# VectorE empties the projections' bank behind the first maximum of the next run in place of in front of it

## Chip, core and metric

The kernel runs on one core of one Trainium2 chip. The metric is the device time of one execution in microseconds (us), the median of several; lower is better. The core's engines work side by side, each through its own list in order, and wait for one another by semaphores: TensorE (PE in the profile, PEld for its weight loads), VectorE (DVE), ScalarE (ACT), GpSimd (POOL), and SyncE's DMA queue (SP).

## What is computed

Four layers of transformer blocks over x of 8 batches x 512 tokens x 256 features, float32. Seven stages hold the first three layers: self-attention (causal), cross-attention, MLP, cross-attention, self-attention with a mask that is loaded, cross-attention, MLP. The last stage is a causal self-attention with 16 heads of 64. The five attention stages that matter here have 16 heads of 16 features and share one form:

```python
h = _ln(x, ln2_g, ln2_b)
q = _heads(_lin(h, q_w, q_b))
k = _heads(_lin(enc_out, k_w, k_b))
v = _heads(_lin(enc_out, v_w, v_b))
a = _attend(q, k, v, causal=False)      # softmax(q k^T * scale) v
x = x + _lin(a, ca_proj_w, ca_proj_b)
```

## The kernel before

An attention stage is cut into 16 units: 8 batches, each in two halves of 8 heads. While one unit's probabilities are computed, the maxima of the next unit's scores are found; its keys, queries and values come from projections that run one or two units ahead. The function `slot(u, ...)` of each engine writes what that engine does in one unit's time, and all engines walk through the same numbered places. A unit has 32 score tiles, k = 0 to 31, in short runs of three (`RUNS[False]`, places r = 0 to 10), or of two in the stage with a loaded mask (`RUNS[True]`, r = 0 to 15).

For each tile TensorE writes the scores for the maximum into one of three banks called `MX` (tile k into bank k % 3), and the scores for the exponential into one of three banks `ST`. VectorE reduces each MX bank to a column of `mx` (L1255 in the cross stages, L1252 in the causal stage, L1248 with the loaded mask, where it also adds the mask to every second ST tile, L1262). TensorE may write MX tile k only when the maximum of tile k - 3 is done, the tiles of the unit before included:

```python
wait(pe, mx_red, TILES * (U if k >= RING else U - 1) + before(k) + 1)
```

Behind the tiles of a run TensorE does jobs at places of a table, `AT`: products with the values (`OUT`), and jobs that all write one single bank, `L`. Each L job waits (`begin`) until the job before it in L has been read out (`l_free`). `K` and `Q` are the key and query projections; ScalarE reads them first (`hi`), then VectorE (`lo`, L1274). `T0` and `T1` turn normalized rows (L618), `M0` and `M1` turn the maxima (L754); ScalarE reads these. In a unit of the second half TensorE projects values at places `V0` and `V1` and VectorE reads them out (`values_out`, L1281, into `V`). In a unit of the first half it projects the attention's output at `O0` and `O1` and VectorE adds them to X (`output_sum`, L1194). For runs of three V0 and O0 lie at place 7, M0 at 8, V1 and O1 at 9, T0 at 10; for runs of two at 11, 9, 13 and 15. So the tile behind V0 and O0 is k = 24, and behind V1 and O1 k = 30 (runs of three) or 28 (runs of two).

Below, "V unit" is a unit with V0 and V1, and "O unit" one with O0 and O1. They take turns. There are 40 of each in the five stages, 80 units with 160 such read-outs.

Of the kernel before, what the change touches and what calls it, by code (L numbers as in the profile page):

```python
# [73 lines left out]
def program(nc, x_in, ctx_in, ctx_rows_in, masks_in, shapes_in, cols_in, rows_in, wts, out):  # L74
# [12 lines left out]
    with es:  # L87
        def sb(name, shape, dt=F32):
            return es.enter_context(nc.sbuf_tensor(name, shape, dt))
# [14 lines left out]
        V = sb("V", [P, 2, NT * H * 32])  # L104
# [114 lines left out]
        def wait(eng, s, v):  # L219

            if not isinstance(v, int) or v > 0:
                eng.wait_ge(s, v)
# [31 lines left out]
        def prob_at(k):  # L254

            return prob[:, k % (4 * G), :]

        def tail_of(s, u):

            return ATTN[s][2], lagged(s, u)  # L260
# [8 lines left out]
        def xt(b, t, n=1):  # L269

            return X[:, bass.ds(NT * b + t, n), :]
# [37 lines left out]
        def a_of(s, u, b):  # L309

            return (s + 1, b + 1 - NB) if isinstance(u, int) and u >= UNITS - 2 else (s, b + 1)

        def m_of(s, u):

            return s + 1 if isinstance(u, int) and u == UNITS - 1 else s

        def end_of(s, u, b):

            return (s - 1, NB - 1) if isinstance(u, int) and u == 0 else (s, b - 1)


        def norm_of(s, u):

            if u == -2:
                return s, 0
            if u % 2 and (u + 1 < UNITS - 2 or s + 1 in JOINED and u < UNITS):
                return a_of(s, u + 1, (u + 1) // 2)
            return None
# [5 lines left out]
        L_NO = {}  # L334
# [835 lines left out]
        def _(dve):  # L1170
            def statistics(N, rows, t):

                if t == 0:
                    wait(dve, ln_mv, NT * N)
                nc.vector.bn_stats(st6[:, t, :], rows).then_inc(ln_stats, 1)

            def combine(N):

                waits(dve, (xh_ready, N), apart=True)
                for t in range(NT):  # L1180
                    waits(dve, (ln_stats, NT * N + t + 1), apart=True)
                    nc.vector.bn_aggr(mv[:, t, :], st6[:, t, :]).then_inc(ln_mv, 1)
# [6 lines left out]
            def layer_norm_x(N, b):  # L1189
                layer_norm(N, lambda t: xt(b, t))  # L1190

            def add_to_x(b, j, bank, done):

                nc.vector.tensor_tensor(xt(b, 2 * j, 2), bank, xt(b, 2 * j, 2), ALU.add).then_inc(done, 1)  # L1194

            def attention(s):
                cross, causal, addmask = ATTN[s]
                n = ATTN_NO[s]

                def slot(u, c, b, p, on):  # L1200
                    half, par = c % 2, c // 2
                    U, GB = UNITS * n + u, NB * n + b
                    sa, _ = a_of(s, u, b)
                    se, be = end_of(s, u, b)
                    norm = norm_of(s, u)
                    if u == UNITS - 2 and on["a"]:
                        prepare(s + 1)
                    if u == -2:
                        layer_norm_x(NB * sa, 0)
                    place = AT[addmask]  # L1210
                    for r, run in enumerate(RUNS[addmask]):
                        for k in run:
                            if on["m"] and k % 16 == 0:
                                wait(dve, max_split, 2 * (U + 1) - 3 + k // 16)
                            if on["m"]:
                                max_tile(m_of(s, u), U + 1, 1 - half, k)
                            if on["b"] and addmask and k % G in BY_VECTOR:
                                add_mask(u, U, k)
                            if on["a"] and k == run[0] and r - 1 in (place["K1"], place["Q"]):
                                low_part(sa, U, half, int(r - 1 == place["Q"]))  # L1220
                        if u != -2 and norm is not None and r < 2:
                            sn, bn = norm
                            if r == 0 and sn > 0:
                                wait(dve, x_done, NB * (sn - 1) + bn + 1)
                            for t in (2 * r, 2 * r + 1):
                                statistics(NB * sn + bn, xt(bn, t), t)
                        if u != -2 and norm is not None and r == place["combine"]:
                            combine(NB * norm[0] + norm[1])
                        if on["tail"] and r == place["invert"] + (tail_of(s, u) == (False, True)):
                            invert(U, 1 - half)  # L1230
                        for part in range(2):
                            if half == 0 and on["op"] and r == place[f"O{part}"]:
                                output_sum((se, be), L_NO[s, u, f"O{part}"], part)
                            if half == 1 and on["a"] and r == place[f"V{part}"]:
                                values_out(sa, u, 1 - par, part)

                def output_sum(end, job, part):

                    dve.wait_ge(l_full, job + 1)
                    add_to_x(end[1], part, Lt, l_free)  # L1240

                def max_tile(sm, U, half, k):
                    _, causal, addmask = ATTN[sm]
                    qt = k % NT
                    waits(dve, (mx_full, TILES * U + k + 1), apart=addmask or causal)
                    bank, m = MXB[k % RING], mx[:, half, k:k + 1]
                    if addmask:
                        nc.vector.tensor_tensor_reduce(bank[:, :], bank[:, :], mask_q[:, qt, :], 1.0, -3.0e38,  # L1248
                                                       ALU.add, ALU.max, m).then_inc(mx_red, 1)
                    elif causal:  # L1250
                        k_n = P * (qt + 1)
                        nc.vector.tensor_tensor_reduce(bank[:, 0:k_n], bank[:, 0:k_n], later0[:, S - k_n:S], 1.0, -3.0e38,  # L1252
                                                       ALU.add, ALU.max, m).then_inc(mx_red, 1)
                    else:
                        nc.vector.tensor_reduce(m, bank[:, :], AX.X, ALU.max).then_inc(mx_red, 1)  # L1255

                def add_mask(u, U, k):
                    i = k // G
                    if k % G == 0:
                        wait(dve, pv_done, 8 * U + i - 3)  # L1260
                    dve.wait_ge(st_full, TILES * U + k + 1)
                    nc.vector.tensor_tensor(prob_at(k), STB[k % RING], mask_k[:, i % 4, :], ALU.add).then_inc(st_masked, 1)  # L1262

                def invert(U, half):

                    for g in range(2):
                        dve.wait_ge(few_in[g], 16 * U)
                    nc.vector.reciprocal(few[:, half, :], few[:, half, :]).then_inc(recip_done, 1)

                def low_part(sa, U, half, kind):  # L1270

                    dve.wait_ge(hi_done, 2 * (U + 2) + kind + 1)
                    at = (C_K, C_Q)[kind] + 2 * ATTN_NO[sa] + half
                    nc.vector.scalar_tensor_tensor(lo[:, kind, :], L[:, :], cols[:, at:at + 1], hi[:, kind, :].bitcast(F32),  # L1274
                                                   ALU.add, ALU.subtract).then_inc(l_free, 1)

                def values_out(sa, u, vpar, j):
                    dve.wait_ge(l_full, L_NO[s, u, ("V0", "V1")[j]] + 1)
                    to = Vh[:, vpar, 2 * j:2 * j + 2, :, :].rearrange("p t h (d two) -> p t h d two", two=2)[:, :, :, :, 0]
                    bias = brow[:, sa % 2, 0:1, :].rearrange("p t (h d) -> p t h d", h=H).broadcast_to([P, 2, H, HD])  # L1280
                    nc.vector.tensor_tensor(to, Lt.rearrange("p t (h d) -> p t h d", h=H), bias, ALU.add).then_inc(l_free, 1)  # L1281

                run_slots(dve, s, slot)

            def mlp(s):
# [180 lines left out]
            def prepare(s):  # L1466

                dve.wait_ge(brow_in[s % 2], brow_count(s))
                if s == CROSS1:
                    quantize()  # L1470
                    dve.wait_ge(quant, QUANT_STEPS)
                scale_queries(s, W[s % 2][:, 0:512], HD ** -0.5)
                if addmask_of(s):
                    dve.wait_ge(masks_loaded, 32)
# [333 lines left out]
```

## Time and profile before

| | us |
|---|---|
| time, median of 3 runs | 4148.82 (4137.39 to 4149.97) |
| span of the profiled execution, first to last instruction | 4128.6 |
| TensorE busy in the span | 3800.3 (92%) |
| VectorE busy | 2734.4 (66%) |
| ScalarE busy | 2398.9 (58%) |
| GpSimd busy | 1660.8 (40%) |

The profiled execution has no time of its own beside its span. The median lies 20.2 us above the span; this is taken as what lies around the instructions. In the span the five attention stages run from about 80 to 1000 us (causal, then cross), from 1220 to 1730 us (cross), to 2290 us (loaded mask) and to 2830 us (cross), the MLPs between them, and the last stage from there to the end. In the rows of a timeline the first two numbers are an instruction's start and its length in us, then engine, line and operation, what it writes and reads, how many are merged, and in brackets how long its engine had been idle and on whom it waited.

### The profile page before, as it was taken

To read this page: it belongs to the slowest core of one execution; us is meant where nothing else is said; L and a number is where in the kernel's file an instruction comes from. 1 tells how busy PE (TensorE), PEld (TensorE's weight loads), DVE (VectorE), ACT (ScalarE), POOL (GpSimd) and SP (SyncE) were. 2 spreads that over 40 slices of the span, in tenths; PEclk is the share of its full clock that TensorE was granted. 3 is DMA by queue.
4 is the path that set the end of the run, shared out by engine and by line. 5 is a ranking of instruction groups with operands and counts; after the bars stand their busy time and mean duration, and the time that the engine had idled before them with its cause. 6 is when DMAs were issued, how large, how long until landed. Compare 5 with 4: busy or idle time off the path is not lost. (4 is left out here: it accounts for less than half of the span.)

```text
span 4128.6 us, 65803 instructions
## 1 busy us (share of the span) xinstructions
PE 3800.3 (92%) x20562; PEld 1962.1 (48%) x20562; DVE 2734.4 (66%) x6813; ACT 2398.9 (58%) x5093; POOL 1660.8 (40%) x1661
## 2 busy tenths in 40 slices
PE   5999999997978999999999999997979999999998
PEld 2444443433873343433333343434855555555555
DVE  4666677774665778789999877784634444444443
ACT  2555567675323676778888867674315555555553
POOL 2333312212321122166767621112326666666664
PEclk8999999998997999989999999998989999999999
DMA  4434344331003534343333354430000000000000
GB/s 101 102 75 81 77 104 85 78 82 40 1 11 59 114 79 86 74 82 64 60 61 61 60 105 84 84 77 34 1 31 6 1 11 12 11 1 12 11 6 11
DMA packets 135499, 220.28 MB, mean 53 GB/s; under 512 B 42736, under 2 KB 45168, under 8 KB 133488
## 3 DMA queue, kind: packets, MB, share of 16 engines
q1 hardware_dynamic: 135152, 216.02, 25.0%
q8 instruction: 173, 2.83, 0.3%
q14 instruction: 174, 1.43, 0.2%
HBM read 59.69 MB, written 5.51 MB: 16 GB/s over the span
## 5 line engine op out<-in xcount | busy, mean ns | idle before, releaser
L1042 ACT ACTIVATE prob<-ST 128x512 f32<-128x512 f32 (+3 forms) x2304 | 1167.1, 565 | 501.9 <-PE ST L608 492.0
L1255 DVE TENSOR_REDUCE mx<-MX 128x1 f32<-128x512 f32 x1536 | 962.6, 681 | 200.6 <-PE MX L608 200.0
L608 PE MATMUL MX<-stk 48*128 48x512 f32 (+3 forms) x2560 | 935.3, 443 | 96.6 <-DVE mx L1255 22.9
L608 PE MATMUL ST<-stk 50*128 50x512 f32 (+3 forms) x2560 | 957.9, 447 | 3.2 <-ACT prob L1042 1.1
L608 PEld LDWEIGHTS MX<-stk 48*128 48x128 f32 x2560 | 426.6, 190 | 784.2 <-DVE mx L1255 321.6
L1654 POOL TENSOR_SCALAR Pr<-Pr,mx 128x128 f32<-128x128 f32 (+3 forms) x512 | 548.3, 1083 | 383.8 <-DVE mx L1416 383.8
L608 PE MATMUL OUT<-prob,V 128*32 128x512 f32 (+3 forms) x5120 | 661.6, 590 | 8.1 <-POOL prob L1617 4.0
L608 PEld LDWEIGHTS ST<-stk 50*128 50x128 f32 x2560 | 431.6, 188 | 57.5 <-ACT prob L1042 23.0
L1527 POOL CAST mhl<-mx 128x16 fp32r<-128x16 f32 x160 | 32.8, 205 | 902.6 <-DVE mx L1255 864.3
L1610 POOL TENSOR_TENSOR prob<-prob,W_odd 128x512 f32<-128x512 f32 x256 | 325.2, 1280 | 120.4 <-ACT prob L1042 120.1
L1248 DVE CUSTOM_DVE_ANT_0 MX<-MX,W_even 128x512 f32<-128x512 f32 x512 | 345.9, 700 | 28.4 <-PE MX L608 28.3
L1052 ACT ACTIVATE prob<-prob 128x512 f32<-128x512 f32 x512 | 305.1, 625 | 2.2 <-POOL prob L1610 1.8
L1252 DVE CUSTOM_DVE_ANT_0 MX<-MX,later 128x128 f32<-128x128 f32 (+3 forms) x512 | 238.1, 516 | 94.0 <-PE MX L608 93.4
L1122 ACT ACTIVATE Pr<-MX,mx 128x128 f32<-128x128 f32 (+3 forms) x256 | 134.9, 527 | 263.3 <-DVE mx L1410 262.8
L1425 DVE COPY PT<-MX 128x128 f32<-128x128 f32 (+3 forms) x256 | 125.5, 490 | 224.2 <-PE MX L881 224.2
L1410 DVE CUSTOM_DVE_ANT_0 MX<-MX,sums 128x128 f32<-128x128 f32 (+3 forms) x256 | 126.9, 496 | 212.4 <-PE ST L608 207.7
L1523 POOL TENSOR_TENSOR X<-X,brow 128x1024 f32<-128x1024 f32 x56 | 132.7, 2370 | 278.5 <-DVE X L1194 278.5
L1029 ACT ACTIVATE hi<-L,cols 128x512 fp32r<-128x512 f32 x160 | 110.0, 688 | 219.5 <-PE L L608 211.4
L608 PE MATMUL L<-W_odd,misc 128*128 128x256 f32 x768 | 200.2, 405 | 22.8 <-POOL misc L1584 21.2
L608 PE MATMUL MX<-QK 64*128 64x128 f32 (+3 forms) x512 | 205.6, 482 | 0.8 <-ACT Pr L1122 0.8
L608 PEld LDWEIGHTS OUT<-prob,V 128*32 128x32 f32 x5120 | 102.0, 109 | 218.7 <-issue 192.8
L608 PE MATMUL ST<-QK 64*128 64x128 f32 (+3 forms) x512 | 205.6, 482 | 0.0
(144 smaller groups left out, 6310.8 us busy)
## 6 DMA issues: line engine op xcount, KB each, us to landing
stk<-hi SPq DMA_DIRECT2D x640, 128.0 KB, 3.9
stk<-lo SPq DMA_DIRECT2D x320, 128.0 KB, 4.0
misc<-misc SPq DMA_DIRECT2D x160, 128.0 KB, 2.6
sums<-spread SPq DMA_DIRECT2D x80, 256.0 KB
misc<-in_ctx_t SPq DMA_DIRECT2D x24, 512.0 KB, 6.9
W_even<-in_w SPq DMA_DIRECT2D x4, 1024.0 KB, 5.5
W_even<-in_w SPq DMA_DIRECT2D x2, 2048.0 KB, 10.1
XH<-in_ctx_rows SPq DMA_DIRECT2D x8, 512.0 KB, 4.6
```

Of the source, the lines that this page charges most:

```text
L608: return nc.tensor.matmul(o, l, r, start=start, stop=stop)
L1042: nc.scalar.activation(prob_at(k)[:, q0:S], STB[k % RING][:, q0:S], ACT.Copy if addmask else ACT.Exp).then_inc(ex_done, 2 if addmask else 1)
L1052: nc.scalar.activation(tile, tile, ACT.Exp).then_inc(late_done, 1)
L1122: nc.scalar.activation(P3(qt, h)[:, 0:k_n], S3[h][t % 2][:, 0:k_n], ACT.Exp, bias=low3[:, qt, h:h + 1], scale=-1.0, accum_out=total3[:, qt ...
L1248: nc.vector.tensor_tensor_reduce(bank[:, :], bank[:, :], mask_q[:, qt, :], 1.0, -3.0e38, ALU.add, ALU.max, m).then_inc(mx_red, 1)
L1252: nc.vector.tensor_tensor_reduce(bank[:, 0:k_n], bank[:, 0:k_n], later0[:, S - k_n:S], 1.0, -3.0e38, ALU.add, ALU.max, m).then_inc(mx_red, 1)
L1255: nc.vector.tensor_reduce(m, bank[:, :], AX.X, ALU.max).then_inc(mx_red, 1)
L1410: nc.vector.tensor_tensor_reduce(bank, bank, later3[:, S - k_n:S], 1.0, 3.0e38, ALU.add, ALU.min, low3[:, qt, h:h + 1]).then_inc(low3_done, 1)
L1425: nc.vector.tensor_copy(to, TP3[1][:, 0:P * (qt + 1)].rearrange("p (k n) -> p k n", n=P)).then_inc(tp3_evac[1], 1)
L1523: nc.gpsimd.tensor_tensor(xt(b, 0, NT), xt(b, 0, NT), bias, ALU.add).then_inc(x_done, 1)
L1610: nc.gpsimd.tensor_tensor(tile, tile, mask_k[:, i % 4, :], ALU.add).then_inc(pool_masked, 1)
L1654: nc.gpsimd.tensor_scalar(tile, tile, inv3[:, qt, h:h + 1], None, ALU.mult).then_inc(nm3_done, 1)
```

## The change

The two read-outs on VectorE are written at another point of the same loop. Before, they stood at the end of place r, behind all the maxima of the run at which TensorE does the projection. Now they stand in the loop over the tiles of place r + 1, behind that run's first tile (and behind its mask addition, where there is one). Nothing else changes: the other four engines have the same lists, and VectorE has the same instructions with the same waits.

```diff
                             if on["a"] and k == run[0] and r - 1 in (place["K1"], place["Q"]):
                                 low_part(sa, U, half, int(r - 1 == place["Q"]))
+                            for part in range(2):
+                                if half == 0 and on["op"] and k == run[0] and r - 1 == place[f"O{part}"]:
+                                    output_sum((se, be), L_NO[s, u, f"O{part}"], part)
+                                if half == 1 and on["a"] and k == run[0] and r - 1 == place[f"V{part}"]:
+                                    values_out(sa, u, 1 - par, part)
...
-                        for part in range(2):
-                            if half == 0 and on["op"] and r == place[f"O{part}"]:
-                                output_sum((se, be), L_NO[s, u, f"O{part}"], part)
-                            if half == 1 and on["a"] and r == place[f"V{part}"]:
-                                values_out(sa, u, 1 - par, part)
```

The order of VectorE in a V unit of a cross stage, from the read-out of the query projection (L1274) to the reciprocal of the next unit, before:

```order
L1274 SCALAR_TENSOR_TENSOR lo<-L,cols,hi 128x512
L1255 TENSOR_REDUCE mx<-MX 128x1 x5
L1281 TENSOR_TENSOR V<-L,brow 128x512
L1255 TENSOR_REDUCE mx<-MX 128x1 x6
L1281 TENSOR_TENSOR V<-L,brow 128x512
L1255 TENSOR_REDUCE mx<-MX 128x1 x14
```

and now:

```order
L1274 SCALAR_TENSOR_TENSOR lo<-L,cols,hi 128x512
L1255 TENSOR_REDUCE mx<-MX 128x1 x6
L1281 TENSOR_TENSOR V<-L,brow 128x512
L1255 TENSOR_REDUCE mx<-MX 128x1 x6
L1281 TENSOR_TENSOR V<-L,brow 128x512
L1255 TENSOR_REDUCE mx<-MX 128x1 x13
```

Each of the two read-outs of V stands one maximum later: behind tile 24 in place of 23, and behind tile 30 in place of 29, one maximum ahead of the unit's last.

The order of VectorE around V0 in the stage with the loaded mask, before (each maximum is a row L1248 on MX with one more for its result):

```order
L1248 ISA MX,mx<-MX,W_even 128x512
L1248 ISA mx 128x1
L1281 TENSOR_TENSOR V<-L,brow 128x512
L1248 ISA MX,mx<-MX,W_even 128x512
L1248 ISA mx 128x1
L1262 TENSOR_TENSOR prob<-ST,W_odd 128x512
L1248 ISA MX,mx<-MX,W_even 128x512
```

and now:

```order
L1248 ISA MX,mx<-MX,W_even 128x512
L1248 ISA mx 128x1
L1248 ISA MX,mx<-MX,W_even 128x512
L1248 ISA mx 128x1
L1262 TENSOR_TENSOR prob<-ST,W_odd 128x512
L1281 TENSOR_TENSOR V<-L,brow 128x512
L1248 ISA MX,mx<-MX,W_even 128x512
```

Here the read-out is moved past two pieces of work, the maximum of tile 24 and the mask addition of tile 24.

## Rows read from the trace of the kernel before

**Rows 1.** The page's head.
```profile
span 4128.6 us, 65803 instructions
```

**Rows 2.** Waits of VectorE, whole span: us in total, times, longest.
```profile
DVE X L1194 <- PE L L608: 130.1, 72, 10.3
...
DVE V L1281 <- PE L L608: 77.6, 64, 2.4
```

**Rows 3.** Waits of TensorE for maxima, whole span, same columns.
```profile
PE MX L608 <- DVE mx L1255: 22.9, 75, 2.7
PE MX L608 <- DVE mx L1252: 17.5, 34, 0.9
PE MX L608 <- DVE mx L1248: 15.9, 43, 0.9
```

**Rows 4.** Windows: stretch, length, busy PE PEld DVE ACT POOL, clock; mask, cross.
```profile
1760.00:2260.00 500.00, 466.23 (x2273) 191.32 (x2274) 462.88 (x1229) 403.87 (x752) 346.71 (x317) 0.93 0.37 66
2400.00:2820.00 420.00, 407.55 (x2326) 167.25 (x2318) 315.44 (x544) 298.94 (x562) 76.49 (x100) 1.00 0.40 82
```

**Rows 5.** Timeline, cross stage, V unit, first tile behind the query projection.
```profile
1406.88 0.49 PE L608 MATMUL MX<-stk 48*128 48x512 f32 x1
...
1407.41 0.69 DVE L1255 TENSOR_REDUCE mx<-MX 128x1 f32<-128x512 f32 x1 [1.14 <-PE MX L608]
```

**Rows 6.** Timeline, the same V unit, from tile 24 to T0.
```profile
1412.36 0.50 PE L608 MATMUL MX<-stk 48*128 48x512 f32 x1
...
1412.47 0.69 DVE L1281 TENSOR_TENSOR V<-L,brow 128x512 f32<-128x512 f32 x1 [0.73 <-PE L L608]
...
1413.08 1.87 DVE L1255 TENSOR_REDUCE mx<-MX 128x1 f32<-128x512 f32 x3
...
1414.25 0.31 PEld L754 LDWEIGHTS L<-ident,mhl 128*8 128x8 f32 x4 [0.84 <-issue]
...
1415.35 0.39 PE L608 MATMUL MX<-stk 48*128 48x512 f32 x1
...
1418.60 0.50 PE L608 MATMUL MX<-stk 48*128 48x512 f32 x1
...
1419.32 1.28 DVE L1255 TENSOR_REDUCE mx<-MX 128x1 f32<-128x512 f32 x2
...
1420.26 0.42 PEld L618 LDWEIGHTS L<-ident,XH 128*128 128x128 f32 x4 [0.84 <-DVE V L1281]
```

**Rows 7.** Timeline, cross stage, the next O unit, from tile 30 on.
```profile
1449.19 1.28 DVE L1255 TENSOR_REDUCE mx<-MX 128x1 f32<-128x512 f32 x2
...
1450.52 0.50 PE L608 MATMUL MX<-stk 48*128 48x512 f32 x1
...
1453.93 0.50 PE L608 MATMUL MX<-stk 48*128 48x512 f32 x1 [0.23 <-DVE mx L1255]
```

**Rows 8.** Timeline, loaded-mask stage, V unit: tile 24, then the next unit's tile 0.
```profile
1985.99 0.50 PE L608 MATMUL MX<-stk 48*128 48x512 f32 x1
...
1993.87 0.46 PE L608 MATMUL MX<-stk 48*128 48x512 f32 x1 [0.33 <-DVE mx L1248]
```

**Rows 9.** Timeline, causal stage: behind Q, tile 30 and T0, O unit's end.
```profile
284.38 0.44 PE L608 MATMUL MX<-stk 48*128 48x384 f32 x1
...
284.85 0.57 DVE L1252 CUSTOM_DVE_ANT_0 MX<-MX,later 128x384 f32<-128x384 f32 x1 [1.60 <-PE MX L608]
...
294.88 0.44 PE L608 MATMUL MX<-stk 48*128 48x384 f32 x1
...
296.06 0.42 PEld L618 LDWEIGHTS L<-ident,XH 128*128 128x128 f32 x4 [0.41 <-DVE V L1281]
...
326.26 0.18 PEld L608 LDWEIGHTS MX<-stk 48*128 48x128 f32 x1 [0.37 <-DVE mx L1252]
```

**Rows 10.** Timeline, the last of the 160 read-outs and the tile at it.
```profile
2797.22 0.50 PE L608 MATMUL MX<-stk 48*128 48x512 f32 x1
...
2797.32 0.69 DVE L1194 TENSOR_TENSOR X<-L,X 128x512 f32<-128x512 f32 x1 [1.50 <-PE L L608]
```

## The prediction

> **What bounds the kernel now.** I read the table of busy time first: TensorE works 92% of the span, VectorE 66%. The windows by stage refine that: in a cross stage TensorE is busy 407.6 of 420 us and VectorE 315.4; in the stage with the loaded mask it is 466.2 of 500 and VectorE 462.9, so there the two lean on each other [rows 4]. TensorE's waits for maxima add up to only 22.9 + 17.5 + 15.9 = 56.3 us [rows 3]: that is all that a better order on VectorE could win, and it lies in many waits of well under a microsecond. A change of VectorE's order can therefore win little, and can lose wherever VectorE becomes late for something that TensorE waits for.
>
> Then the waits of VectorE: it waits for the value projection at 64 of its 80 read-outs of V, 77.6 us, and for the output projection at 72 of 80, 130.1 us [rows 2]. At these places VectorE has nothing else to do, and the projection is what arrives last. The timeline shows the place in detail. TensorE ends V0 and goes on with MX tile 24 at 1412.36; VectorE begins the read-out at 1412.47, 0.11 us later, and the three maxima at 1413.08 [rows 6]. I followed this through all 160 read-outs of the timeline: each begins 0.10 or 0.11 us behind the start of the tile that follows the projection, the last one too, 2797.32 against 2797.22 [rows 10]. So at no place is VectorE behind when the projection's result is there.
>
> **What the change does at each place.** The read-out now has to wait for the maximum of the tile behind the projection. When is that tile ready? Its product must come through first. The nearest row is the tile behind the query projection, where TensorE also comes from a long job in L: tile started 1406.88, maximum started 1407.41, 0.53 us later [rows 5]. Before, VectorE was at work 0.11 us behind the tile's start; now it starts 0.53 us behind it. The sum of work is the same, maximum plus read-out. So VectorE idles **0.42 us** more, and everything behind the pair is 0.42 us later. In the causal stage tile 30 has 384 columns; there the maximum starts 284.85 - 284.38 = 0.47 us behind [rows 9], and the lag is 0.47 - 0.10 = 0.37 us.
>
> What is gained in return: the first maximum itself ends earlier. It began at 1413.08 and begins at 1412.36 + 0.53 = 1412.89 now, 0.19 us sooner. The one who waits for it is MX tile 27, whose run's last tile starts only at 1415.35 [rows 6]; it does not wait, so I put the gain at 0.
>
> What is lost besides: the bank L comes free later. The read-out ended at 1412.47 + 0.69 = 1413.16. Now it starts one step of a maximum, 0.61 us (1413.08 - 1412.47), behind 1412.89, at 1413.50, and ends at 1414.19, 1.03 us later. A release reaches TensorE 0.05 us later (maximum ended 1449.19 + 1.28 = 1450.47, tile 1 started 1450.52) [rows 7].
>
> The Trainium skill ("PSUM — Partial Sum Buffer", the summary of rules for kernel authors) says to empty PSUM promptly. Read strictly, as if each late release were paid in full, it would make 160 x 1.03 = 165 us. The rows below let most of that pass, since the next job in L is seldom there so soon.
>
> **Cross stages, V unit** (24 of them). M0 starts at 1414.25 [rows 6]; the release comes at 1414.19 + 0.05 = 1414.24, in time with no margin. The maximum of tile 26 ended at 1413.08 + 1.87 = 1414.95, now 1415.37; tile 29 at 1415.35 waits for it until 1415.42: **0.07**. Behind V1, tile 30 then starts at 1418.60 + 0.07 = 1418.67, its maximum at 1419.20, the read-out at 1419.81, its end is 1420.50, the release 1420.55. T0 would start at 1420.26 [rows 6]: TensorE is late by **0.29 us** in all, since between V1 and T0 only two tiles and one product lie. V units: 24 x 0.29 = 7.0 us.
>
> **Cross stages, O unit** (24). No T0 follows, but the next unit's tile 1 goes into the bank of tile 31. Its maximum ended at 1450.47, now 0.07 + 0.42 later at 1450.96, the release is at 1451.01 against 1450.52: 0.49. Not all stays: at 1453.93 TensorE had waited 0.23 us for a maximum, because VectorE has the layer norm's statistics there [rows 7]. TensorE's own chain takes up that wait, and 0.49 - 0.23 = 0.26 is left: 24 x 0.26 = 6.2 us.
>
> **Causal stage** (8 and 8). V unit: tile 30 at 294.88, its maximum at 295.35, the read-out one 384-column step later, which I take as 0.47 too, at 295.82, its end 296.51, the release 296.56; T0 started at 296.06 [rows 9]: 0.50, so 4.0 us. O unit: tile 1 of the next unit already waits 0.37 us for the maximum of tile 31 [rows 9]; what that is late by (0.37) comes on top: 3.0 us. The lag behind V0 and O0 I put at nothing here, as the short tiles leave VectorE waiting for TensorE before tile 27.
>
> **Loaded-mask stage** (8 and 8). Tile 24 starts at 1985.99 behind V0, its maximum can start at 1986.52. The lag of 0.42 is not paid twice: VectorE arrives 0.42 late at V1, and so finds tile 28 ready. At the unit's end TensorE waits 0.33 us for VectorE (1993.87) [rows 8], so a later VectorE is a later TensorE: 0.42 x 16 = 6.7 us. The read-out's own lateness is larger here, as a mask addition goes in front as well, but the next job in L is two runs away.
>
> **Sum:** 7.0 + 6.2 + 4.0 + 3.0 + 6.7 = 26.9 us. The profiled span of 4128.6 [rows 1] would become 4155.5; the median lies 20.2 us above the span and should keep that, so 4148.8 + 26.9 = **4176 us**, 0.65% slower. A difference under 0.3%, 12.4 us, is about what a measurement of this kernel can't tell from none.
>
> Bounds: if every one of the 160 places cost its 0.42 us, it would be 67 us (4216). If only the 32 T0 waits of V units cost something (24 x 0.29 + 8 x 0.50 = 11 us), it is 4160. I hold to the sum since its terms are each read at a place that repeats with the same distances.
>
> **Rivals.**
> 1. *The lag is absorbed.* VectorE idles a third of the span, and much of the 0.42 us falls in front of waits that it has anyway. For it: M0 and tile 27 are reached with hardly a loss. Against it: T0 has only 0.29 us less than it needs but at a fixed distance, and no slack lies between. Then the time is 4149 to 4160. Chance 0.12.
> 2. *The first maximum is what counts, and the kernel gets faster.* A bank MX is freed 0.19 us sooner at 160 places; if TensorE waited for that very maximum at each, it would win 160 x 0.19 = 30 us (4118). It decides from the point where TensorE reaches tile 27 (or the next unit's tile 0 behind tile 30) before that maximum ends. At the places read it comes 1 us or more after. Chance 0.03.
> 3. *The clock reacts.* In the cross window TensorE was granted 1.00 of its clock, with 97% busy; in the mask window 0.93, with 93% busy [rows 4], that is the level of 1.2 in place of 2.4 GHz for 14% of the time, which costs half of that. The new waits of 0.3 to 0.5 us per 30 us take about 1% of busy time. If the three cross stages (some 1450 us) fell a third of the way, to 0.98, it would cost 29 us on top: 4205. Chance 0.10. The Trainium skill ("TensorE: Matmul & The Clock Gate", what's actually happening) describes a clock that is throttled by default and released by activity; by it alone waits as short as these should not let it fall, which is why this isn't the forecast.
> 4. *The change does nothing*, because VectorE's order stays: excluded by the two orders shown.
>
> **How the numbers follow.** My forecast, slower by 13 to 50 us with 27 as the likeliest, has a chance of 0.75, the rivals 0.12, 0.03 and 0.10. Faster by over 0.3%: 0.03. Within 0.3%: 0.12. Slower by over 0.3%: 0.85. The range takes most of the forecast, reaches down to rival 1's upper end and up towards the clock's case: 4158 to 4202.
>
> **What would show it in the profile of the changed kernel.** VectorE's waits for the L projection at L1281 and L1194 nearly vanish, and waits of L1255 and L1248 for TensorE's MX tiles grow by about the same. Read-outs begin some 1.14 us behind tile 24 in a cross stage. TensorE's waits at L618 for V (L1281) appear with about 0.2 to 0.5 us each in the V units, and its waits of MX tiles for maxima grow from 56 us by some 10 to 20. The clock in the cross window stays 1.00. The forecast is wrong if T0 starts as soon as before, which would mean that a tile's maximum can start sooner than 0.53 us behind it, or if the clock's windows fall.

## The result, and the profile after

The changed kernel takes 4194.26 us (median of 4 runs, 4183.4 to 4206.8); the kernel before took 4143.91 us beside it on the same chip (4 runs, 4137.39 to 4149.97). The ratio is 1.0124 [1.0099, 1.0150]: slower by some 50 us, where 27 had been forecast. The page's head, and below it TensorE's waits that answer to [rows 3] (us in total, times, longest):

```profile
span 4185.8 us, 65803 instructions
PE 3832.3 (92%) x20562; PEld 1967.0 (47%) x20562; DVE 2732.5 (65%) x6813; ACT 2404.8 (57%) x5093; POOL 1664.2 (40%) x1661
```

```profile
PE MX L608 <- DVE mx L1255: 26.0, 79, 2.7
PE MX L608 <- DVE mx L1252: 23.4, 40, 0.9
PE MX L608 <- DVE mx L1248: 22.8, 41, 1.5
...
PE L L618 <- DVE V L1281: 8.7, 26, 1.1
```

The waits for maxima grew from 56.3 to 72.2 us, and a wait that was hardly there (0.2 us, once) is new: T0, the transposes at L618, waits 26 times for the read-out of V. VectorE's own waits, the answer to [rows 2]:

```profile
DVE mx L1255 <- PE MX L608: 324.7, 269, 6.5
...
DVE MX L1252 <- PE MX L608: 170.9, 128, 6.1
...
DVE MX L1248 <- PE MX L608: 53.2, 59, 5.1
...
DVE X L1194 <- PE L L608: 25.1, 4, 10.5
```

The 64 waits of L1281 for the projection are gone from the list and those of L1194 have shrunk from 72 to 4. The waits of the maxima for their tiles have grown instead: L1255 from 200.0 to 324.7 us, L1252 from 93.4 to 170.9. The wait has changed its name and become longer. The 4 that are left are all 25.1 us of L1194's list: they stand at the last output projections in front of the two MLPs (1031.33, 1034.11, 2892.42 and 2895.20 us), which have no score tile behind them. So the order changes at 156 of the 160 read-outs.

The place itself, in a cross stage, V unit, to be laid beside [rows 5] and [rows 6] (timeline: start and length in us, engine, line; in brackets the idle time ahead and who ended it):

```profile
1442.73 0.50 PE L608 MATMUL MX<-stk 48*128 48x512 f32 x1
1443.26 0.69 DVE L1255 TENSOR_REDUCE mx<-MX 128x1 f32<-128x512 f32 x1 [1.15 <-PE MX L608]
1443.87 0.72 DVE L1281 TENSOR_TENSOR V<-L,brow 128x512 f32<-128x512 f32 x1
1444.49 3.10 DVE L1255 TENSOR_REDUCE mx<-MX 128x1 f32<-128x512 f32 x5
1444.64 0.31 PEld L754 LDWEIGHTS L<-ident,mhl 128*8 128x8 f32 x4 [0.86 <-DVE V L1281]
...
1445.83 0.18 PEld L608 LDWEIGHTS MX<-stk 48*128 48x128 f32 x1 [0.36 <-DVE mx L1255]
1445.84 0.50 PE L608 MATMUL MX<-stk 48*128 48x512 f32 x1
1446.27 1.06 PE L608 MATMUL OUT<-prob,V 128*32 128x512 f32 x8
...
1449.19 0.50 PE L608 MATMUL MX<-stk 48*128 48x512 f32 x1
1449.72 0.69 DVE L1255 TENSOR_REDUCE mx<-MX 128x1 f32<-128x512 f32 x1 [2.13 <-PE MX L608]
1450.33 0.68 DVE L1281 TENSOR_TENSOR V<-L,brow 128x512 f32<-128x512 f32 x1
1451.06 0.42 PEld L618 LDWEIGHTS L<-ident,XH 128*128 128x128 f32 x4 [1.06 <-DVE V L1281]
```

(L1281 is the read-out of V, L754 is M0, L618 is T0.) Tile 24 starts at 1442.73; the maximum starts 0.53 us behind it and the read-out 1.14 us behind it, as forecast. M0 (L754) starts 1.91 us behind tile 24, where it was 1.89 before: no loss, but the one that it now waits for is the read-out. Tile 29 starts 3.11 us behind, 2.99 before: 0.12 us of wait. And what follows it pays once more, a restart of 0.10 us: from tile 29 to the product behind it (OUT) it is 0.43 us (1445.84 to 1446.27), where it was 0.33 (1415.35 in [rows 6] to 1415.68 below). T0 starts 8.33 us behind tile 24, 7.90 before: 0.43 us lost in one V unit. Three more rows of the kernel before, of the same unit, to compare with; the first two serve in an experiment below:

```profile
1408.76 0.50 PE L608 MATMUL MX<-stk 48*128 48x512 f32 x1
...
1410.44 1.99 PE L608 MATMUL L<-W_odd,misc 128*128 128x256 f32 x8
...
1415.68 1.06 PE L608 MATMUL OUT<-prob,V 128*32 128x512 f32 x8
```

From the 160 read-outs of the timeline I took the length of each stage and from the trace's clock the time that lies at the lower level in each, called half clock below (1.2 in place of 2.4 GHz). In the kernel before the stretches run between the read-outs at 69.85, 492.38 and 963.37 us (causal, first cross) and at 1348.26, 1774.37, 2349.80 and 2797.32 us; after the change they run between the same read-outs:

| stage | before, us | after, us | at half clock, before and after |
|---|---|---|---|
| causal | 422.5 | 443.3 | 34 and 75 |
| cross, first | 471.0 | 479.6 | 7 and 14 |
| cross, second | 426.1 | 432.3 | 3 and 7 |
| loaded mask | 575.4 | 588.1 | 79 and 82 |
| cross, third | 447.5 | 452.6 | 3 and 3 |

The rest of the program grew by 4 us. TensorE is at half clock for 388 us in all, where it was 333. What a microsecond at half clock costs, the runs show: over the 171 timed runs of all kernels here, one kernel's run with a mean clock lower by 0.001 is 2.5 us longer. A microsecond at half clock lowers that mean by 0.5/4150 = 0.00012, so it costs about 0.30 us; that this is less than the half that the level alone would make is probably because TensorE waits in part of it anyway. The mean clock of the changed kernel's runs is 0.951 and of the kernel before 0.957 to 0.958; by this slope some 17 us of the 50 are clock, and some 33 are lag.

The windows of the causal stage and of the first cross stage, first before, then after (columns as in [rows 4]: the clock is the third number from the right):

```profile
110.00:490.00 380.00, 346.77 (x2221) 171.85 (x2220) 253.04 (x980) 213.19 (x530) 142.91 (x209) 0.96 0.43 84
520.00:980.00 460.00, 446.33 (x2549) 183.90 (x2546) 351.36 (x608) 325.39 (x614) 83.89 (x112) 1.00 0.39 83
```

```profile
110.00:490.00 380.00, 346.09 (x2133) 168.80 (x2132) 242.21 (x947) 203.45 (x505) 141.85 (x202) 0.92 0.39 81
520.00:980.00 460.00, 444.21 (x2510) 181.37 (x2507) 357.50 (x624) 316.31 (x600) 91.63 (x121) 0.99 0.41 85
```

In the same 380 us of the causal stage TensorE is busy for as long as before and gets through 4% fewer instructions. In the cross stage the clock is nearly as it was, 0.99 and 1.00.

### The profile page after: what moved, and what is told of

It reads as the page before. It is cut to its first block and busy times, and to the rows that moved or that the text cites. A ratio compares the mean times of both kernels' runs of the same rounds, so it can differ in the third digit from the quotient of the medians.

```text
span 4185.8 us, 65803 instructions
## 1 busy us (share of the span) xinstructions
PE 3832.3 (92%) x20562; PEld 1967.0 (47%) x20562; DVE 2732.5 (65%) x6813; ACT 2404.8 (57%) x5093; POOL 1664.2 (40%) x1661
## 5 line engine op out<-in xcount | busy, mean ns | idle before, releaser
L1255 DVE TENSOR_REDUCE mx<-MX 128x1 f32<-128x512 f32 x1536 | 969.4, 683 | 337.9 <-PE MX L608 324.7
L608 PE MATMUL MX<-stk 48*128 48x512 f32 (+3 forms) x2560 | 953.3, 448 | 108.5 <-DVE mx L1255 26.0
L608 PE MATMUL ST<-stk 50*128 50x512 f32 (+3 forms) x2560 | 969.3, 450 | 3.8 <-ACT prob L1042 1.7
L1248 DVE CUSTOM_DVE_ANT_0 MX<-MX,W_even 128x512 f32<-128x512 f32 x512 | 347.1, 702 | 53.8 <-PE MX L608 53.2
L1252 DVE CUSTOM_DVE_ANT_0 MX<-MX,later 128x128 f32<-128x128 f32 (+3 forms) x512 | 239.6, 516 | 171.0 <-PE MX L608 170.9
```

The source lines that it names most:

```text
L608: return nc.tensor.matmul(o, l, r, start=start, stop=stop)
```

## The experiments

Each is the kernel before with one edit, of which the lines that matter are shown, shortened; "moved" means that the read-out stands behind the first maximum, as in the change. Ratios are to the kernel before on the same chip, with the 95% interval; its median was 4147.14 us in the first group (22 runs), 4148.92 in the second (25) and 4147.11 in the third (23).

### Which stage pays

```diff
+def MOVED(s, half, part): return s == SELF0       # e1: the causal stage alone
+def MOVED(s, half, part): return s in CROSS_NO    # e2: the three cross stages
+def MOVED(s, half, part): return s == SELF2       # e3: the loaded-mask stage
...
+                            for part in range(2):     # behind the first maximum of the next run
+                                if MOVED(s, half, part) and half == 1 and on["a"] and k == run[0] and r - 1 == place[f"V{part}"]:
+                                    values_out(sa, u, 1 - par, part)      # and output_sum in the same way
...
-                            if half == 1 and on["a"] and r == place[f"V{part}"]:
+                            if not MOVED(s, half, part) and half == 1 and on["a"] and r == place[f"V{part}"]:
                                 values_out(sa, u, 1 - par, part)
```

Expected of the causal stage alone:

> The read-outs are moved in the causal stage alone; the other four attention stages keep the old order. Lag theory (each read-out waits for its tile, 0.37 to 0.42 us, and only what TensorE waits for counts): 7 us slower than before, within 0.3%. Clock theory (the lag is small, but the new short waits make the granted clock fall more often in this stage, where the changed kernel had 75 us at half clock against 34 before): 17 to 25 us slower, and the mean clock of this stage again clearly below before's 0.96. If the clock's difference was only the luck of one execution, the stage's clock is near 0.96 again.

Of the cross stages:

> The read-outs are moved in the three cross stages alone. Lag theory: each pair of units is longer by 0.77 us, as in the trace of the changed kernel, 24 pairs: 15 to 19 us slower, at a clock of 0.99 to 1.00 in these stages. Clock theory: nothing more here, since the cross stages kept their full clock in the changed kernel. A rival by which the loss lies at the borders between stages would leave this kernel within 8 us of before.

Of the loaded-mask stage:

> The read-outs are moved in the stage with the loaded mask alone. Lag theory as forecast: 0.42 us a unit, 7 us. The trace of the changed kernel had 12.7 us more in this stage with nearly the same time at half clock (79 to 82 us), so if the lag costs more there than forecast (VectorE is the busiest here) it is 11 to 13 us. Clock theory: more than that, with more time at half clock.

| moved in | median, us | ratio | us of it | mean clock |
|---|---|---|---|---|
| causal stage | 4166.33 | 1.0040 [1.0020, 1.0060] | 17 | 0.954 |
| cross stages | 4163.96 | 1.0038 [1.0024, 1.0052] | 16 | 0.958 |
| mask stage | 4159.06 | 1.0029 [1.0015, 1.0044] | 12 | 0.954 |

The three add up to 44 us (0.0107), against 51 (0.0124) for all, within the intervals. The cross stages do nearly what was forecast (13.2) and leave the clock alone. The causal stage costs more than twice its 7.0, the mask stage nearly twice its 6.7, and both with a lower clock: by the slope above 9 of the causal stage's 17 us, and nearly all of the mask stage's, are clock; the slope times so small a difference is good to some 5 us. The window of the causal stage in the first of these kernels:

```profile
110.00:490.00 380.00, 345.14 (x2106) 167.28 (x2106) 240.29 (x941) 201.95 (x502) 141.10 (x200) 0.92 0.39 80
```

and of the second, which leaves this stage as it was:

```profile
110.00:490.00 380.00, 345.92 (x2181) 170.32 (x2180) 250.59 (x971) 211.32 (x523) 142.18 (x207) 0.95 0.41 83
```

So the lower clock of the causal stage follows the edit in that stage. For the mask stage one profile decides nothing: where it is untouched it is 575.4 us long before, but 590.9 in the first of these kernels and 588.9 in the second, as long as after the change.

### Is it the wait for the tile?

```diff
+def ahead(r, k):  # run r is a V or O projection that moves, k the first tile of run r + 1
-                            if on["m"]:
+                            if on["m"] and not ahead(r - 1, k):
                                 max_tile(...)
...
+                        if on["m"] and ... ahead(r, RUNS[lag][r + 1][0]):   # ahead of the projection
+                            max_tile(ATTN[m_of(s, u)][1], U + 1, 1 - half, RUNS[lag][r + 1][0])
```

TensorE makes the MX tile ahead of the projection, so that it is long there when VectorE comes; all 160 read-outs are moved.

> VectorE's order as in the changed kernel, and TensorE computes the MX tile that the moved read-out stands behind in front of the projection in place of behind it (all five stages, both parts). Lag theory: the tile's maximum is then done while the projection runs, the read-out starts as soon as the projection ends, so the 0.42 us at each place is gone and nearly all of the 50 us with it: back to before's time or up to 10 us under it, less what TensorE newly waits for the bank in front of the projection at part 0, about 0.3 us at 80 places (up to 24 us). Expected 4130 to 4165. If the loss came from anything but the wait for the tile (for instance that bank L is read out behind a maximum at all), it stays near 4190.

It took 4202.44 us, 1.0131 [1.0108, 1.0154]: a miss. Its timeline at V0:

```profile
1403.16 0.49 PE L616 MATMUL MX<-stk 48*128 48x512 f32 x1
...
1403.81 0.49 PE L616 MATMUL MX<-stk 48*128 48x512 f32 x1
...
1404.40 0.50 PE L616 MATMUL MX<-stk 48*128 48x512 f32 x1
...
1405.00 0.50 PE L616 MATMUL MX<-stk 48*128 48x512 f32 x1
1405.43 1.59 PEld L616 LDWEIGHTS L<-W_odd,misc 128*128 128x128 f32 x8 [0.25 <-issue]
...
1407.36 0.50 PE L616 MATMUL ST<-stk 50*128 50x512 f32 x1
1407.36 0.50 PE L616 MATMUL MX<-stk 48*128 48x512 f32 x1
...
1407.46 0.69 DVE L1209 TENSOR_TENSOR X<-L,X 128x512 f32<-128x512 f32 x1 [0.72 <-PE L L616]
...
1408.24 0.16 PEld L616 LDWEIGHTS OUT<-prob,V 128*32 128x32 f32 x8 [0.36 <-issue]
```

The part of the theory that speaks of VectorE holds: the read-out starts 0.10 us behind the tiles that follow the projection, as in the kernel before. But the tile ahead costs a place of its own. The tiles ahead of the projection come 0.59 to 0.65 us apart, which is VectorE's step of one maximum (0.61): TensorE gets each bank only when a maximum has emptied it. One tile more there is 0.60 us more (2.27 us from the first tile to the projection, 1.68 before, from 1408.76 to 1410.44). And behind the projection nothing is saved: an MX product and its ST product start within 0.01 us of each other and take one place together, so with the MX product gone the ST product still takes it (0.88 us from 1407.36 to OUT for the run of three, 0.90 before, from 1412.36 to 1413.26). The experiment had put a new cost in place of the old one. So in the next kernels the ST product goes ahead too:

```diff
+                            if on["b"]:                                  # beside max_tile, ahead of the projection
+                                score_tile(U, half, RUNS[lag][r + 1][0])
+def AHEAD(s, half, part): return True        # e8: all 160;  e9: part == 1, read-outs of part 1 moved alone
```

> As e4_tile_ahead (VectorE's order as in the changed kernel; TensorE computes the tile that the read-out stands behind in front of the projection), but both products of that tile go ahead, the MX one and the ST one, at all 160 places. In e4's trace the ST product left behind took 0.33 us alone, as long as the two did together, since they start at the same time. If that separation was e4's cost, this one wins 0.3 us at each of 160 places back, 30 to 50 us: 4150 to 4175. What stays is the wait for the bank in front of part 0 (0.2 to 0.3 us at 80 places) and 0.1 for each new start. If it stays near 4200 the cost of e4 was the bank's wait alone, and the separation cost nothing.

> The same pair ahead of the projection at part 1 only (V1 and O1), VectorE's read-out moved at part 1 only; part 0 as before. There a product with the values stands between the run and the projection, so the bank is free (no wait). The last maximum of a unit is done about 0.6 us sooner, which removes the wait of the next unit's tile 1 (0.2 to 0.4 us in O units). Cost: 0.1 us for a new start at 80 places, 8 us; gain 5 to 12 us. Expected 4138 to 4155, no difference that can be measured; clearly faster than before would make it the best order.

The first took 4156.75 us, 1.0022 [1.0002, 1.0042], with the clock at 0.960; the second 4155.57 us, 1.0007 [0.9992, 1.0022]. So with all 160 read-outs moved, but the tile there in time, 0.0102 of the 0.0124 is gone, some 42 us. The waits are gone too: TensorE's waits for maxima add up to 55.8 us again (56.3 before, 72.2 in the changed kernel), and T0's wait for the read-out is this:

```profile
PE L L626 <- DVE V L1304: 0.4, 1, 0.4
```

This supports the wait for the tile as the cause of the lag, but the 42 us are not its price. By the slope 23 of them are clock (0.960 against 0.951). And in the cross stages, at full clock, this kernel is not the faster one: a V unit and an O unit together are 1.11 us longer than before there, and 0.78 in the changed kernel (the table below). What the tile ahead newly costs there, the wait for a bank in front of the projection and more single starts, is more than the wait that it takes away. It wins in the causal and the mask stage (429.1 and 568.7 us, against 443.3 and 588.1). No version here beats the kernel before, even without that wait.

### Which read-outs pay

```diff
+def MOVED(s, half, part): return part == 0                  # e5: V0 and O0
+def MOVED(s, half, part): return part == 1                  # e6: V1 and O1
+def MOVED(s, half, part): return half == 1 and part == 1    # e11: V1 alone
+def MOVED(s, half, part): return half == 0 and part == 1    # e12: O1 alone
```

> Only the first read-out of each unit (V0 and O0, 80 places) is moved behind the next run's first maximum; V1 and O1 stay. Lag theory with the durations of the changed kernel's trace: the last tile of the run behind M0 waits 0.12 us and its restart costs 0.1 more, 0.2 us a place in the cross stages (48: 10 us), some 0.4 in the causal stage (16: 6 us), nothing net in the mask stage, where the lag of V0 is the same as that of V1: 0.42 a unit (16: 7 us). Together about 20 us, of which the clock may add 5. Rival (only T0 and the next unit's tile 1 matter, as the forecast had it): 3 to 8 us in the cross and causal stages, within 0.3% in all.

> Only the second read-out of each unit (V1 and O1, 80 places) is moved. Lag theory: T0 late by 0.22 and tile 1 of the next unit, 0.15 to 0.25 us a place in the cross stages (48: 9 us), 0.4 to 0.5 in the causal one (16: 7 us), 0.42 a unit in the mask stage, alone as well as with part 0 (7 us); 23 us, and 5 to 10 from the clock. So the two halves of the change together (this and e5) should cost more than the whole by about the mask stage's 7 us. If the parts were independent everywhere, they add up to the whole, 48 us.

> Only the second read-out of V (V1, 40 places) is moved, the one behind which T0 waits for the bank L. Theory: T0 is late by 0.24 us in the cross stages (24 units, 6 us), by 0.5 in the causal one (8, 4 us), and 0.42 a unit in the mask stage (8, 3 us): 13 us and something for the clock, which the four changed causal and mask pieces drew so far with 8 to 15 us. Of e6's 36 us this should be half or more.

> Only the second read-out of the output projection (O1, 40 places) is moved. No job in L waits for it; the maximum of tile 31 is late for the next unit's tile 1. Theory: 0.15 to 0.26 us in the cross stages (24, 4 to 6 us), 0.37 in the causal one (3 us), 0.42 in the mask stage (3 us): 10 to 12 us and something for the clock.

| moved | median, us | ratio | us of it | mean clock |
|---|---|---|---|---|
| V0, O0 | 4162.76 | 1.0024 [1.0003, 1.0044] | 10 | 0.956 |
| V1, O1 | 4187.90 | 1.0087 [1.0065, 1.0109] | 36 | 0.950 |
| V1 | 4164.97 | 1.0041 [1.0022, 1.0061] | 17 | 0.954 |
| O1 | 4161.46 | 1.0039 [1.0023, 1.0054] | 16 | 0.954 |

Halves add up again: 10 + 36 = 46, 17 + 16 = 33 of 36. In time three quarters of the cost lies with the later read-out of each unit, but some 14 us of that difference is clock (0.950 against 0.956). The lag by itself can be read in the second cross stage, at four pairs of units where every kernel has its full clock. From the read-out of one V0 to that of the next it is 59.16 us in the kernel before, and longer by this:

| | longer by, us | forecast |
|---|---|---|
| V0, O0 moved | 0.40 | 0.14 |
| V1, O1 moved | 0.37 | 0.41 |
| V1 moved | 0.23 | 0.22 |
| O1 moved | 0.16 | 0.19 |
| all moved (the change) | 0.78 | 0.55 |
| all moved, tile and score product ahead | 1.11 | |
| V1, O1 moved, tile and score product ahead | 0.41 | |

The parts add up to the whole (0.40 + 0.23 + 0.16 = 0.79). V1 and O1 cost what was forecast for T0 and for the next unit's tile 1. V0 and O0 cost as much as they do, 0.2 us each, which is the wait of 0.12 at tile 29 and the start of 0.10 behind it.

### The opposite move, and the clock

VectorE has one other step that reads a bank of L behind such a tile: the low part of K and Q (L1274), which stands behind the first maximum in both kernels. Here it is put in front, and nothing else is changed:

```diff
-                            if on["a"] and k == run[0] and r - 1 in (place["K1"], place["Q"]):
-                                low_part(sa, U, half, int(r - 1 == place["Q"]))
+                        if on["a"] and r in (place["K1"], place["Q"]):
+                            low_part(sa, U, half, int(r == place["Q"]))
```

> The old order for V and O. In its place the read-outs of the key and query projections (the low part, L1274), which the kernel before has behind the next run's first maximum, are put in front of it in all five stages. There VectorE must wait for ScalarE's high part, which is done 0.8 us behind the start of the tile (ScalarE starts at 1406.98 and takes 0.69, the tile started at 1406.88), while the tile's maximum can start 0.53 behind. Theory (the one that is ready first goes first): VectorE then idles 0.3 us more at each of 160 places and is late for the tiles behind; 15 to 40 us slower. Rival (a read-out is best in front, since the bank comes free sooner, and behind is bad everywhere): faster than before by several us.

It took 4220.33 us, 1.0169 [1.0148, 1.0190], some 70 us more; the direction was as expected, the size was not. Two rows of its waits, and its timeline at Q:

```profile
DVE lo L1274 <- ACT hi L1029: 265.9, 160, 15.4
...
PE MX L608 <- DVE mx L1255: 51.6, 157, 3.8
```

```profile
1394.74 0.50 PE L608 MATMUL MX<-stk 48*128 48x512 f32 x1
...
1394.84 0.69 ACT L1029 ACTIVATE hi<-L,cols 128x512 fp32r<-128x512 f32 x1 [1.23 <-PE L L608]
...
1395.57 0.75 DVE L1274 SCALAR_TENSOR_TENSOR lo<-L,cols,hi 128x512 fp32r<-128x512 f32 x1 [1.44 <-ACT hi L1029]
1396.23 3.67 DVE L1255 TENSOR_REDUCE mx<-MX 128x1 f32<-128x512 f32 x6
```

Here ScalarE must first write the high part, from 0.10 to 0.79 us behind the tile's start, so L1274 can start only 0.83 us behind it. The maximum could have started at 0.53 [rows 5]; now it starts at 1.49. At this place the maximum is what is ready first, and behind the V and O projections it is the bank `L`. Both kernels that put the step that is ready later in front are slower, by 51 us (160 times 0.32) and by 70 us (160 times 0.44).

The last kernel asks for the clock alone: the order of the kernel before, but T0 of the causal stage waits as it has to in the changed one, until the unit's last maximum:

```diff
+                            if s == SELF0 and on["m"]:          # in T0
+                                pe.wait_ge(mx_red, TILES * (U + 2))
```

> VectorE's order is that of the kernel before everywhere. Only in the causal stage, TensorE's job T0 also waits for the maximum of tile 31, which by the trace of before ends 0.8 us behind T0's start (296.86 against 296.06): a plain wait on TensorE, eight times, about 6 to 7 us in all, as large as the lag that the change was forecast to cause in this stage (7 us). Clock theory: such waits alone lower the granted clock of the stage, so the time grows by 12 to 20 us, and the stage's clock is under 0.93 as in e1 rather than 0.96. If the clock is moved by something else in the changed order, the loss is 5 to 8 us at before's clock.

It took 4155.07 us, 1.0021 [1.0006, 1.0035], 9 us more, with the mean clock at 0.958, and its causal window is this:

```profile
110.00:490.00 380.00, 343.70 (x2196) 168.90 (x2193) 251.25 (x979) 211.26 (x523) 143.38 (x206) 0.96 0.41 84
```

A wait in front of T0 is paid with its own length and the clock stays as it was. By stages, in single profiles: the causal stage has 59 us at half clock here, 34, 48 and 52 in the kernel before and the two that move read-outs in other stages alone, 75 in the changed kernel and 93 where it alone is changed. So "each new wait lowers the clock" falls as a theory.

The traces of all these kernels show where the clock does fall. This kernel's wait lies in the V units; the falls that the change adds lie in the O units. Take the first six O units of the causal stage in each profile. Where the read-out of O1 waits for its tile (the changed kernel, and the ones that move the causal stage, V1 and O1, or O1 alone), the clock goes to the lower level for 3.41 us, beginning 4.4 to 5.1 us behind the start of the tile that follows O1, in 4, 6, 4 and 5 of the six: 19 of 24. In the ten other profiles it does so at that place in 0 of 60, and among them are the three with the tile ahead. One O unit of each kernel follows: a row of the timeline (tile 1 of the next unit), then two windows, the first from the start of the tile behind O1 and the second as long as a fall. Before:

```profile
326.26 0.38 PE L608 MATMUL MX<-stk 48*128 48x256 f32 x1
...
324.23:328.67 4.44, 4.15 (x36) 2.16 (x36) 4.16 (x14) 2.88 (x7) 1.06 (x3) 1.00 0.53 118
328.67:332.08 3.41, 3.37 (x19) 1.22 (x16) 3.17 (x18) 2.75 (x7) 1.42 (x3) 1.00 0.16 53
```

and after the change:

```profile
401.86 0.38 PE L608 MATMUL MX<-stk 48*128 48x256 f32 x1 [0.61 <-DVE mx L1252]
...
399.50:403.94 4.44, 3.82 (x33) 1.90 (x32) 3.75 (x14) 2.60 (x7) 1.07 (x3) 1.00 0.54 118
403.94:407.35 3.41, 3.41 (x19) 1.37 (x18) 3.41 (x18) 3.08 (x8) 1.13 (x2) 0.50 0.13 43
```

TensorE is held for 0.61 us ahead of tile 1 of the next unit and is busy for 3.82 in place of 4.15 us, and then the clock falls. From the tile behind O1 to the tile behind the next V0 it is 20.35 us in the kernel before at full clock, 20.67 to 20.69 with O1 moved and no fall, and 21.68 to 21.74 with one fall: 0.33 us of lag, and 1.0 us for 3.41 us at half clock, the slope's 0.30 for each once more. Why the clock answers to the wait at this place and not to others of that length is not shown, nor what lowers it in the mask stage, where the changed kernel's profile has 82 us at half clock against 79 before, but the kernel with this stage alone changed 133.

## Why the prediction was right, and where it was off

The sign and the mechanism of the lag held, and the lag alone, some 33 us, is near the 27 of the sum. The whole was some 50, near the range's upper end: it lies inside because the range had been stretched up towards the clock's case, which had a chance of 0.10 and came beside the lag, in other stages than that rival named. One of the prediction's own signs of being wrong did appear: a window of the clock fell, from 0.96 to 0.92 in the causal stage. By its own steps:

- **The lag of 0.42 us per place** is right to 0.01 us: maximum 0.53 and read-out 1.14 us behind tile 24. That it is the cause in the cross stages is shown by the partial moves, which cost there what the late release or the late maximum makes, and by the waits, which go when tile and score product are there in time. It works at 156 places, not at 160: the row that [rows 10] calls the last read-out is followed by two more, and those and two others have no tile behind them.
- **The gain on the first maximum is nothing**, and the late release of L costs nothing at M0 (1.91 us behind tile 24 against 1.89): right. The order was worth some 50 us in all, clock included, not the 165 that paying each release in full would make.
- **Cross stages, V unit, 0.29 us**: measured 0.43. Of the term for tile 29, 0.07 in the forecast, the wait is 0.12, and what was not in the sum is the restart: the pair of products at tile 29 takes 0.43 in place of 0.33 us. I had taken tile 29's delay as a shift of the rest, and it is a shift and a restart. This is the step of the sum that was too small in the cross stages: 0.07 for what V0 or O0 costs, and 0.20 measured.
- **Cross stages, O unit, 0.26 us**: from one V0 to the next, V and O unit together, the period grew by 0.77 to 0.80 us where 0.55 was forecast, so some 0.35 for the O unit: 0.16 of it for O1 (0.19 forecast), the rest for O0. Cross stages together: 24 times 0.77 is 18.5 us; moved alone, they cost 16 [10, 22]; the forecast's 13.2 is in that interval.
- **Causal stage, 7.0 us**: this is the largest miss, 17 [8, 25] moved alone, 20.8 in the one pair of profiles, and the step that failed is the clock, which the sum did not have: 75 us at half in place of 34, at 0.30 us each 12 us of the 20.8. What is left, 8 us, is near the forecast's 7.0, and its parts are right: from tile 24 to tile 30 TensorE takes 5.49 us at full clock before and after, so the lag behind V0 and O0 is nothing here, as said (the read-outs themselves come 0.4 us further apart, 0.58 us behind their tile at V0 and 0.96 at V1); and the O unit costs 0.33 where 0.37 was forecast.
- **Mask stage, 6.7 us**: moved alone it cost 12 [6, 18], mostly with the clock. The lag shows in the units at full clock: from the tile behind O1 to that behind the next V0 it is 30.64 us in the changed kernel and 30.19 to 30.21 in kernels that leave O1 as it was (the stage's last unit left aside), 0.44 where 0.42 was forecast. And it is not paid twice, as said: from tile 24 to tile 28 it is 4.41 us in both.
- **Rival 3, the clock reacts**: it was given 0.10 and placed in the cross stages. It came with some 17 us, and in the other places, where the clock was below 1.00 already. The reason against it was taken from a window at 1.00 and said nothing of one at 0.96. The Trainium skill's rule ("TensorE: Matmul & The Clock Gate", what's actually happening), a clock that is throttled by default and released by activity, had made me expect no fall behind waits as short as these. In the cross stages the trace agrees, with some 11 us more at half clock in all three; in the causal stage it does not, where the clock fell behind a wait of 0.61 us.
- **Rivals 1 and 2** fall: nothing near a full absorption (4149 to 4160), and nothing near 4118. T0 starts later, as was said would decide it.
- **The base.** "The median lies 20.2 us above the span and should keep that" was a wrong reading, though it did no harm: only 1.7 us lie around the span (4187.54 and 4185.8 in the profile after). The profiled execution before was simply at the short end of the scatter: with 1.7 us on top it is 4130.3 us, and 70 later runs lie between 4130.67 and 4161.88, with 4147 as the mean. It is also why the two spans shown differ by 57 us and the medians by 50.
- **The signs named in the profile**: read-outs 1.14 us behind the tile, the new waits of L618 and the vanished ones of L1281 and L1194 came as said; the waits for maxima grew by 16 us (10 to 20 forecast).

## What to carry to other kernels

Where an in-order engine has two steps to do and both come free at nearly the same time, put first the one whose input is there first, and read that from the start times in the timeline: here some 0.4 us at each of some 160 places decided, in one direction for V and O and in the other for K and Q. Where a forecast adds up delays of a pipelined engine, give each new wait its restart as well as its length, and price the clock stage by stage, beginning with the stages where it is below its full level already. Read a lag from the tiles of the engine that bounds the kernel, at full clock, and not from the read-outs that were moved: their distances change with the move. A step that is moved ahead to take away a wait may take a place in a stretch that another engine paces: look at what sets the distance of its neighbours before it is moved.

## What was not expected of the hardware

- Two products of 48 and of 50 rows, into two banks, start within 0.01 us of each other and take one place together; without its partner one of them still takes that place. Taking the MX product alone out of a run of three saved 0.02 us.
- Such a pair costs 0.10 us more when it doesn't start close behind another pair. In a run of three at full clock the starts are 0.33, 0.23 and 0.33 us apart (1412.36, 1412.70, 1412.93, OUT at 1413.26). A single pair is followed 0.43 us later, behind a wait for a bank (1445.84 to 1446.27) and without one too, as here in the kernel with the pair ahead at all places:

```profile
1432.84 0.50 PE L616 MATMUL MX<-stk 48*128 48x512 f32 x1
...
1433.28 1.07 PE L616 MATMUL OUT<-prob,V 128*32 128x512 f32 x8
```

- A microsecond of TensorE at 1.2 in place of 2.4 GHz costs 0.30 us of this kernel's time, from the slope over 171 runs. One fall of 3.41 us in an O unit of the causal stage costs 1.0 us, the same price. The falls come back at the same place of the unit, 4.4 to 5.1 us behind the tile that follows O1, in 19 of 24 units with the wait there and in 0 of 60 without it; waits of 9 us in all that were put in front of T0 brought none there.
